# GpSimd's chain released earlier, masks moved up, a ones product removed and a new order for the drain, in a graph attention layer followed by a Mamba-2 block

## The reference, cut to what matters

```
# graph part, on xn = layernorm(x)
e    = leaky_relu(xn @ a1 + (xn @ a2).T, 0.2);  U = softmax(where(adj > 0, e, -9e15))
feat = soft_threshold(mix of xn, U @ xn and xn * rowsum)      # rowsum = sum(0.5 * U * U)
x1   = x + mix of feat, U @ feat, rowsum and h0
# Mamba-2 block, on layernorm(x1); 32 chunks of 128 rows, 4 heads of 64, state 64
z, xBC, dt = split(x @ W_in);  xBC = silu(causal conv of 4 taps);  dt = softplus(dt + dt_bias)
dA = dt * A;  A_cum = cumsum(dA in the chunk);  L = exp(segsum(dA))
Y  = (C B^T * L) @ (x * dt) + C @ state * exp(A_cum) + D * x
state = state * exp(A_cum[last]) + B^T @ (x * dt * exp(A_cum[last] - A_cum))
out = x1 + rmsnorm(Y * silu(z)) @ W_out @ W_lin + b_lin
```

## Time and profile before

| | |
|---|---|
| median of 3 runs | 808.99 us (808.49 to 809.42) |
| the profiled execution's own time | 808.94 us |
| its span, first to last instruction | 807.2 us |
| TensorE, VectorE, ScalarE, GpSimd busy | 94%, 92%, 84%, 72% of the span |
| mean granted TensorE clock | 0.970 |

### The profile page before, as it was taken

One profiled execution on the slowest core, in us unless ns is written; L12 is line 12 of the kernel. 1 busy time (PEld: TensorE's weight loads), 2 busy tenths in 40 slices (PEclk: granted clock), 3 DMA queues, 4 the chain that ended last, 5 costly groups with the idle time before them and its releaser, 6 DMA issues. The chain is left out here.

```text
span 807.2 us, 20951 instructions
## 1 busy us (share of the span) xinstructions
PE 756.7 (94%) x6079; PEld 721.4 (89%) x6079; DVE 739.7 (92%) x1934; ACT 675.4 (84%) x1428; POOL 582.9 (72%) x1115
## 2 busy tenths in 40 slices
PE   3689999999999999869999999999999999999976
PEld 1389999999999999868899999999999999999955
DVE  6999999999999999796999999999999999999872
ACT  5989898989989897865888888888898989888761
POOL 5683667776777677856888878788787878788850
PEclk9989999999999999979999999999999999999975
DMA  7689897989889794122111121112121212110000
GB/s 212 191 257 328 267 326 242 336 259 325 273 302 291 258 308 184 29 53 81 56 55 66 44 67 44 65 42 68 42 69 39 68 39 68 46 37 14 5 8 10
DMA packets 97961, 110.43 MB, mean 137 GB/s; under 512 B 6865, under 2 KB 89713, under 8 KB 97905
## 3 DMA queue, kind: packets, MB, share of 16 engines
q1 hardware_dynamic: 97906, 109.78, 41.9%
HBM read 90.87 MB, written 18.89 MB: 136 GB/s over the span
## 5 line engine op out<-in xcount | busy, mean ns | idle before, releaser
L1271 ACT ACTIVATE maskA<-code 128x1024 fp32r<-128x1024 int8 x256 | 269.0, 1053 | 24.9 <-DVE code L762 21.4
L1609 PE MATMUL accA<-Y,maskA 128*128 128x260 f32 (+1 forms) x1792 | 270.6, 294 | 8.9 <-ACT maskA L1271 6.1
L1618 PE MATMUL accC<-Y,maskC 128*128 128x260 f32 (+1 forms) x1792 | 254.6, 285 | 2.6 <-DVE maskC L770 2.6
L1609 PEld LDWEIGHTS accA<-Y,maskA 128*128 128x128 f32 x1792 | 232.6, 191 | 14.4 <-issue 7.8
L1618 PEld LDWEIGHTS accC<-Y,maskC 128*128 128x128 f32 x1792 | 230.6, 191 | 3.6 <-DVE maskC L770 3.6
L770 DVE TENSOR_SCALAR maskC<-code 128x1024 fp32r<-128x1024 int8 x256 | 206.5, 808 | 0.0
L762 DVE SCALAR_TENSOR_TENSOR code<-f_rows,neg_f,ps 128x512 int8<-128x512 int8 (+1 forms) x256 | 177.9, 737 | 0.4 <-DVE neg_f L726 0.2
L1208 ACT ACTIVATE edges<-adj_in 128x1024 int8<-128x1024 f32 x128 | 135.2, 1059 | 1.5 <-DMA adj_in<-in_adj_dram 1.5
L625 POOL TENSOR_TENSOR room_r<-room,room_r 128x256 fp32r<-128x256 f32 x128 | 95.6, 774 | 2.5
L1044 DVE SCALAR_TENSOR_TENSOR room<-room 128x128 f32<-128x128 f32 x279 | 89.5, 342 | 0.0
L1550 PE MATMUL ps<-ident,edges 128*128 128x128 bf16 x512 | 51.2, 224 | 10.2 <-ACT edges L1208 10.2
(11 more groups left out here) (260 smaller groups left out, 1620.9 us busy)
## 6 DMA issues: line engine op xcount, KB each, us to landing
adj_in<-in_adj_dram SPq DMA_DIRECT2D x128, 512.0 KB, 5.0
edge_codes<-code SPq DMA_DIRECT2D x32, 512.0 KB, 5.5
code<-edge_codes SPq DMA_DIRECT2D x32, 512.0 KB, 3.2
xn<-in_x_dram SPq DMA_DIRECT2D x4, 512.0 KB, 5.6
room<-in_x_dram SPq DMA_DIRECT2D x32, 64.0 KB, 1.8
room<-in_L_gnn_h_dram SPq DMA_DIRECT2D x32, 64.0 KB, 1.9
out_dram<-room SPq DMA_DIRECT2D x32, 64.0 KB, 1.6
room<-in_L_ffn_W_in_dram SPq DMA_DIRECT2D x1, 192.0 KB, 2.5
```

The costliest lines, as they stand in the source:

```text
L1271: s.activation(maskA[:, b % MASKS], src, ACT.Relu, bias=1.0 - LINK, scale=-1.0).then_inc(S["maskA_ready"], 1)
L1609: t_.matmul(accA[k][:, 0:2 * cols], maskA[:, b % MASKS, l * P:(l + 1) * P], y2_of(jt, 0) if cols == F else Y[:, jt, 0, :, 0:cols], start=j ...
L1618: m = t_.matmul(accC[k][:, 0:2 * cols], maskC[:, b % MASKS, l * P:(l + 1) * P], y2_of(jt, 1) if cols == F else Y[:, jt, 1, :, 0:cols], sta ...
```

## The change

- A semaphore `taken` counts when GpSimd's `features` has read a tile's sums; `read_acc` and `sum1` of round one wait for it in place of `scaled_done`.
- Masks 4 and 5 of round two are made in the middle, ahead of the last `Y2` tiles; `FIRST` has (1, 2) before (0, 3); `feat1(29)` moves behind the features of the last two tiles, which are formed in `acc_s` and no longer in `scaled`, because `scaled` still holds tile 29's.
- The product with `ones` (`L1732`) goes. GpSimd forms exp(A_cum[last]) as exp(A_cum) of a row times that row's decay to the end, from `expD`. ScalarE's exponentials wait for `ps_ready` one tile later.
- The drain's order changes on all four engines; `decays` is split in two, `convolve` in three, `read_inputs` in two.

```
-        FIRST = [(0, 0), (0, 1), (0, 2), (1, 0), (1, 1), (0, 3), (1, 2), (1, 3)]
+        FIRST = [(0, 0), (0, 1), (0, 2), (1, 0), (1, 1), (1, 2), (0, 3), (1, 3)]
 load_codes (SP)
-  taken = ... + (2 if T == SLOTS else 0)
+  taken = ... + (3 if T == SLOTS else 0)
 features (GpSimd)
                 link(g.tensor_tensor(num[:], ps_sum[:, k, 0], ps_sum[:, k, 1], ALU.add))
+                g.sem_inc(S["taken"], 1)
 read_acc, sum1 (round one)
-                    wait(act, "scaled_done", T - 1)
+                    wait(act, "taken", T - 1)
 decayed_state (GpSimd)
+                link(g.tensor_tensor(tiny[0:DS, 15, 0:NH], tiny[0:DS, 4 + kc, 0:NH], expD[0:DS, :, P - 1], ALU.mult))
                 g.tensor_tensor(heads(pstate[0:DS], HD), heads(state[0:DS, kc], HD),
-                                tiny[0:DS, 4 + kc, NH:2 * NH].unsqueeze(2).broadcast_to([DS, NH, HD]), ALU.mult)
+                                tiny[0:DS, 15, 0:NH].unsqueeze(2).broadcast_to([DS, NH, HD]), ALU.mult)
 cumulate (TensorE)
-                t_.matmul(ps[2][:, NH:2 * NH], ones[:], da, start=True, stop=True)
 middle (VectorE)
             mask2(2, 0, 2)
-            for t in Y2_AT[BLOCKS]:
-                y2_low(t)
+            y2_low(NT - 8)
             sum1(NT - 1, 1)
...
             mask2(3, 0, 3)
...
-            feat1(NT - 3, 1)
...
+            mask2(4, 1, 0)
             (k_T times xn, two tiles)
+            y2_low(NT - 7)
...
             v.tensor_tensor(xn[:, two, :], fwork[:], both_T, ALU.subtract).then_inc(S["last_feat"], 1)
+            y2_low(NT - 6)
+            dve.wait_ge(S["last_feat"], 1)
+            feat1(NT - 3, 1)
+            mask2(5, 1, 1)
+            for t in range(NT - 5, NT):
                 y2_low(t)
 middle (ScalarE): y2_high(24), read_acc(31), y2_high(25), mask 3, y2_high(26), (27), mask 4, (28), mask 5, (29) to (31)
 decays (ScalarE)
+            def exp_decays(c, kc):
+                act.wait_ge(S["p_cum"], c + 1)
+                wait(act, "y_read", c - 1)
+                wait(act, "ps_ready", c)
+                s.activation(tiny[:, 4 + kc, 0:NH], ps[2][:, 0:NH], ACT.Exp)
+                wait(act, "mix_ready", c)
+                s.activation(expD, ...).then_inc(S["exp_done"], 1)
+            def x_times_dt(c, kc):
+                act.wait_ge(S["p_cum"], c + 1)
+                wait(act, "p_s", c)
+                (four products, as before)
 y_state (VectorE)
                 dve.wait_ge(S["p_y"], c + 1)
+                wait(dve, "yg_ready", c)
```

More of the change, by code:

```diff
@@ L667, in drain @@
             def drain():
[L668 to L679, removed]
+                a, b, c, d = range(LAST - 3, NT)
+                second_rstd(d)
+                decayed_state(a, a % 2)
+                split_dam(c, c % 2)
+                x1_with_bias(c, c % SLOTS)
+                decayed_state(b, b % 2)
+                norm_scale(a)
+                decayed_state(c, c % 2)
+                split_dam(d, d % 2)
+                x1_with_bias(d, d % SLOTS)
+                norm_scale(b)
+                norm_scale(c)
+                norm_scale(d)
                 end_chain()
@@ L784, in sum1 @@
                 dve.wait_ge(S["acc_read"], T + 1)
-                wait(dve, "scaled_done", T - 1)
+                wait(dve, "taken", T - 1)
                 both = accC[k][:, 0:2 * XC].rearrange("p (a b) -> p a b", a=2)
@@ L1154, in drain @@
             def drain():
[L1155 to L1164 removed]
+                a, b, c, d = range(LAST - 3, NT)
+                made_c, made_d = {}, {}
+                dve.wait_ge(S["p_o"], a)
+                summed = sum_parts(d, d % 2)
@@ new lines, in drain @@
+                make_xbc(d, d % 2)
+                output(a, a % 2, a % SLOTS)
+                make_gate(c, c % 2)
+                off = y_state(c, c % 2)
+                mix(d, masked_g(d))
+                y_within(off)
+                output(b, b % 2, b % SLOTS)
+                y_gated(c, c % 2)
+                make_gate(d, d % 2)
+                y_within(y_state(d, d % 2))
+                y_gated(d, d % 2)
+                output(c, c % 2, c % SLOTS)
+                output(d, d % 2, d % SLOTS)
@@ L1410, in read_inputs @@
                     s.copy(hist[:, 1 - kc, :, 0:TAPS - 1], hist[:, kc, :, P:P + TAPS - 1]).then_inc(S["halo_done"], 1)
+            def read_inputs(c, kc, between=None):
+                copy_z(c)
+                if between is not None:
+                    between(c)
+                copy_xbc(c, kc)
             def exp_logit(c):
@@ new lines, in drain @@
+                b_times_c(b, b % 2)
+                pe.wait_ge(S["in_read"], c + 1)
+                inputs(d)
+                outputs_y(b, b % 2)
+                contribution(b)
+                cumulate(c, c % 2)
+                b_times_c(c, c % 2)
+                turn_y(a)
+                outputs(a)
+                outputs_y(c, c % 2)
+                contribution(c)
+                cumulate(d, d % 2)
+                b_times_c(d, d % 2)
+                pe.wait_ge(S["out_done"], a + 1)
```

270 lines of the change are left out of this document (144 added, 126 removed).

## The result

The changed kernel takes 802.29 us (median of 15 runs, 799.77 to 807.25), the kernel before 807.96 us beside it (804.79 to 809.81): ratio 0.9933, 95% interval 0.9916 to 0.995. It is faster, by 5.7 us and not by the 13.7 forecast, and lies outside the range of 791.5 to 800.5. Its profiled execution took 803.38 us, the span 801.7.

The account below looks back on a forecast made before the run. The tensor engine was taken to bound round two's loop, and chains of waits between engines its two ends. Gains of 6.4 (loop), 2.8 (middle) and 4.5 (drain), 13.7 off 808.99, gave 795.3 us; 8-in-10 range 791.5 to 800.5.

Parts of the forecast that it names:

- part 2: End of round one: `taken` for `scaled_done` removes ScalarE's 2.05 us wait and brings `sum1(31)` 2.6 us earlier.
- Part 2 and 3, the middle: Round one to round two: earlier sums, masks and reordered products bring `sum_parts(0)` forward 2.8 us, between 2.2 and 3.6.
- so it is kept: From `sum_parts(0)` to round two's steady loop: the same chain runs as before, so the 2.8 us gain stays whole.
- Part 1, the ones product: Round two's loop: dropping it saves 0.22 us of tensor queue in 29 slots, 6.4 us; GpSimd's replacement product is hidden.
- Rival A: Round two's loop: VectorE becomes the bound, slots take 13.05 us, the part gives 3.8, time 797.9 us; chance 0.13.
- Part 4, the drain: The drain: c's outputs precede `cumulate(d)`, d's exponential follows at once, 3.5 us earlier; gain 4.5 us, bounds 0 and 8.
- Rival B: The drain gives nothing, as the late start of c and d is not made good; 799.8 us, chance 0.17.

Follow-up runs that it names:

- inc_only: The kernel before, with only the semaphore increment added behind the sums in GpSimd's features and nobody waiting for it; 813.3 us, ratio 1.0058.
- inc_late: inc_only with the increment moved to the end of GpSimd's chain, behind the increment of `scaled_done`; 808.81 us, ratio 0.9996.
- taken_last: The changed kernel with the increment only in tiles 28 and 29 and the waits for it only in tiles 30 and 31; 795.57 us, ratio 0.9849.
- warm_8: taken_last with 8 matmuls of no use on the tensor engine ahead of slot 2 of round two; 795.16 us, ratio 0.9842.
- ones_only: The kernel before without the ones product, GpSimd's small product in its place, nothing else changed; 802.53 us, ratio 0.9924.
- after_again: The changed kernel itself run once more, with a trace of its own; 800.63 us, ratio 0.9895 against the kernel before.
- no_product: ones_only without GpSimd's small product, so the state's scale leaves out the tile's decay; 803.69 us, ratio 0.9944.
- drain_only: The kernel before with the new order of the drain alone, ones product and `scaled_done` kept; 805.76 us, ratio 0.9948.
- middle_only: The kernel before with masks 4 and 5 early, (1, 2) before (0, 3) and `feat1(29)` moved back, `scaled_done` kept; 809.12 us, ratio 1.0004.
- scaled_after: The changed kernel with round one waiting for `scaled_done` again and no `taken` increment; 797.4 us, ratio 0.9852.

## Why the prediction was wrong

**The step that failed** is part 2: "At the end of round one ScalarE's wait of 2.05 us goes and `read_acc(31)` is no longer late." That is what happened at the end of round one; but `taken` is counted in every tile, and no term stood for the increment in GpSimd's chain: round one's loop was put at nothing without a row of it. Its rows show 99.6 and 99.2% busy engines and a chain that ends just ahead of VectorE's sum, so the chain had little room. With the increment it is 0.47 us longer, and sum(29) comes 4.6 us later. Shown by inc_only (+4.5 to sum(29), nothing elsewhere), by inc_late (the same instruction behind the chain costs nothing) and by taken_last, which has it in two tiles and takes 795.57 us (795.22 to 798.78) where the forecast was 795.3. Of the chain's 0.47 us, 0.11 is the increment's own gap. The other 0.36 is the net of GpSimd instructions that now take longer, as `L537` with 0.89 us for 0.34, and others that take less; which instruction collides with which I did not take apart.

**Part 2 and 3, the middle: "so it is kept" failed, as a second step.** To sum_parts(0) the gain was as sized: 2.57 us (2.73 in taken_last) for 2.8. The tensor engine, though, ran out of work 3.5 us before the first transpose, and the clock fell behind that stop and not ahead of it, where the kernel before had it (0.50 from 353 to 363). The new low stretch lies on the chain: 1.3 us in taken_last, 2.7 in the first trace. warm_8 fills the stop and takes back all of the 1.3.

**Part 1, the ones product:** right. 0.22 us was read, 0.20 a slot measured, 5.2 to 5.4 us in 26 slots (ones_only, taken_last, after_again) where 5.7 was in the sum; the missing part is in every fourth slot, at 13.1. The Trainium skill (TensorE: Matmul & The Clock Gate, Back-to-back issue gap) gives 81 ns a pair of weight load and matmul for 128 columns, where these matmuls have 4. By it an estimate is 26 x 0.16 = 4.2; these traces show 0.10 to 0.11 a pair. The first trace's 4.19 comes from its two long slots and does not bear that estimate out. The product on GpSimd cost the tensor engine nothing that shows in most slots, as worked out. Rival A did not come: VectorE still waits 0.47 us a slot for ScalarE.

**Part 4, the drain:** the mechanism right in its two main steps (c's outputs before `cumulate(d)`, the exponential directly behind). Counted from c=29, the exponential of d starts 5.0 us earlier than before, where 3.5 was forecast, and from it to the last output it takes 10.1 us, where 11.1 was kept. The stage varies from trace to trace, with either order. With the old order and the ones product c=29 to the end took 54.36, 54.33, 52.95 and 50.47 us, mean 53.0; with the new order and without the product 47.31 to 49.20 over seven traces, mean 48.0. That is 5.0 us, where the forecast has 4.5 + 0.7. The share of the order alone is smaller: without the ones product the old order took 49.80 and 51.37 us (ones_only, no_product), 2.6 more than the 48.0; with it the new order took 48.98 (drain_only), 4.0 less than the 53.0, and 4.2 by the ratio. The 6.04 between the two first traces is more than the change gives; how much of the spread is the clock, which fell at other places in each trace, stays open. The block of GpSimd's multiply, which the prediction did not have, costs 0.7 us where it falls.

**Sum.** Without the increment's term the sum comes close, in part by luck: in taken_last the span is 13.5 us shorter (-0.14 to sum(29), 2.73 to sum_parts(0), -1.35 to c=3, 5.29 in the loop, 6.97 to the end), the loss behind sum_parts(0) made up by a drain that is long in the trace of before. By the ratio, 0.9849 of some 808 us, the gain is 12.2 us (10 to 14), not 13.7, and the parts one by one give 6.1 (ones_only), nothing (middle_only) and 4.2 (drain_only). Between the two medians of the changed kernel (802.29 and 800.63) the ratio differs too, 0.9933 and 0.9895 with intervals that barely touch; beyond the long slots of one trace (1.1 us together) nothing here explains it. Rival B's 799.8 lies nearest to the result, but its reason did not come: the drain did give.

## What to carry to other kernels

Ahead of a diff's gain, look at every loop that it adds an instruction to, even a bare count, and ask of the engine's chain there how long before its reader it ends: here some 27 tiles at 0.17 us cost as much as the middle and half the loop gave. Signal an early read only in the iterations that wait for it. When a stop of the tensor engine is moved, look at what runs behind its new place, for here the low clock moved with it.

## What the runs showed of the hardware

A semaphore increment that stands by itself in this chain of GpSimd widened the gap between two instructions by 0.11 us (0.10 to 0.21); at the end of the chain it cost nothing that shows (inc_late, 0.9996).

A GpSimd multiply of 64 x 256 takes 0.61 us where it is not held up (as for the tiles ahead of it in all these traces), and up to 3.73 beside nine VectorE taps with two inputs in SBUF, which then take 2.43 instead of 4.41: it can be held over several of VectorE's instructions. The Trainium skill (SBUF — State Buffer, Who interferes with whom) says that such instructions contend and that the order of issue decides who blocks. The first the traces bear out. The second they leave open: in all these traces VectorE's mixing instruction was running when the multiply began, and the taps were issued after the multiply, yet with the multiply 0.12 us behind the start of the mix it took 3.72 us (after) and with 0.11 it took 1.03 (scaled_after). The ends of instructions on GpSimd are rough in a profile, so a difference of hundredths there is not to be read.

Less work on GpSimd went with a longer loop (no_product against ones_only, 2.7 us) and with more of VectorE's masks stretched beside GpSimd's products. That the one brings the other is likely, and not shown. Without that one small product every fourth slot took 13.5 us, not 13.1.

The clock fell behind a stop of 3.5 us of the tensor engine in taken_last (granted 0.76 from 370 to 375 us) and stayed at 1.00 there when 16 weight-and-matmul pairs filled the stop (warm_8), for no work of use.
